# The scan's skip connection on VectorE instead of TensorE in a Mamba-2, attention and mixture-of-experts block

## What is computed

```python
def step(h, inp):                        # per head: 4 heads of 64 channels, 64 states
    x_t, dt_t, B_t, C_t = inp
    dA = jnp.exp(dt_t * A)
    h = h * dA[:, :, None, None] + (dt_t[:, :, None] * x_t)[..., None] * B_t[:, None, None, :]
    y = jnp.einsum('bhpn,bn->bhp', h, C_t)
    return (h, y)
...
y = jnp.moveaxis(ys, 0, 1) + xs * D[None, None, :, None]     # the skip connection
y = y.reshape(Bt, L, D_INNER)
y = y * jax.nn.silu(z)
y = y * jax.lax.rsqrt(jnp.mean(jnp.square(y), axis=-1, keepdims=True) + EPS) * norm_w
return y @ out_proj_w.T
```

## Time and profile before

| | |
|---|---|
| three runs, median (lowest to highest) | 913.11 us (911.67 to 915.75) |
| profiled execution | 912.75 us, of which the span from first to last instruction 911.0 us |
| mean granted PE clock in the span | 0.967 of 2.4 GHz |
| busy: PE, DVE, ACT, POOL | 796.8, 632.1, 502.1, 300.3 us |
| `diag_d` products on PE | 128 records, 22.9 us busy |
| `xdt` products on DVE (L1458) | 32, 13.6 us busy |

### The profile page before, as it was taken

How to read it: one execution, slowest core, us unless ns; L and a number is a source line. 1 busy time by engine, 2 the same in 40 slices (tenths; PEclk the granted TensorE clock), 3 DMA queues, 4 the chain that set the end, 5 groups by cost and what they waited for, 6 DMA issues and landing times.

```text
span 911.0 us, 17953 instructions
## 1 busy us (share of the span) xinstructions
PE 796.8 (87%) x5396; PEld 473.8 (52%) x5396; DVE 632.1 (69%) x1491; ACT 502.1 (55%) x960; POOL 300.3 (33%) x566
## 2 busy tenths in 40 slices
PE   3549999998999889998999899998999989998887
PEld 1324454745547455654546455464556546464545
DVE  1675468784888748885697847886588856977523
ACT  2324675465843675456754667436754567446552
POOL 4322606044231614135150542316151351405300
PEclk9756999999999999999999999999999999999979
DMA  4000000000000000000000000000000000000000
GB/s 157 1 8 12 15 1 1 8 14 24 0 1 6 25 11 0 7 12 24 0 0 7 13 23 0 1 17 24 0 0 7 12 24 0 0 7 13 24 0 12
DMA packets 15144, 11.72 MB, mean 13 GB/s; under 512 B 1040, under 2 KB 13968, under 8 KB 14992
## 3 DMA queue, kind: packets, MB, share of 16 engines
q1 hardware_dynamic: 15120, 11.43, 4.2%
HBM read 7.76 MB, written 2.10 MB: 11 GB/s over the span
## 4 chain that ended last, share of the span: by engine, by line
PE 56%; DVE 17%; issue 12%; ACT 8%; POOL 6%; DVEq 1%; POOLq 0%; ACTq 0%
PE R L443 38%; PE S L443 13%; DVE sb_mx L1176 6%; DVE sb_x L1422 2%; POOL sb_pr L1690 2%; POOL sb_lnv L1595 2%; PE S L448 1%; DVE sb_tokqk L1359 1%; PE R L561 1%; PE R L448 1%; ACT sb_es L1114 1%; ACT L943 1%; ACT sb_junk L989 1%; DVE sb_st L1200 1%; DVE sb_yc L1480 1%
## 5 line engine op out<-in xcount | busy, mean ns | idle before, releaser
L1079 ACT ACTIVATE sb_pr<-S 128x768 f32<-128x768 f32 (+1 forms) x192 | 165.6, 887 | 152.3 <-PE S L443 151.2
L1176 DVE TENSOR_REDUCE sb_mx<-S 128x2 f32<-128x256 f32 (+3 forms) x256 | 198.0, 817 | 37.8 <-PE S L443 35.7
L1690 POOL TENSOR_SCALAR_AFFINE_SELECT sb_pr<-sb_pr 128x256 f32<-128x256 f32 (+1 forms) x192 | 97.0, 507 | 339.6 <-ACT sb_pr L1079 337.6
L443 PE MATMUL R<-sb_pr,sb_va 128*32 128x512 f32 (+3 forms) x1024 | 89.7, 445 | 19.6 <-POOL sb_pr L1690 19.6
L443 PE MATMUL S<-sb_maskb,sb_identb 128*128 128x128 bf16 (+1 forms) x384 | 51.4, 249 | 32.8 <-DVE sb_mx L1176 30.2
L443 PEld LDWEIGHTS S<-sb_maskb,sb_identb 128*128 128x128 bf16 x384 | 27.8, 101 | 100.3 <-DVE sb_mx L1176 83.6
L443 PE MATMUL R<-sb_xfT,sb_W 128*128 128x512 f32 x144 | 75.9, 635 | 3.3 <-ACT sb_pr L943 3.3
L443 PE MATMUL R<-sb_W,sb_pr 128*128 128x96 f32 (+1 forms) x512 | 70.9, 279 | 0.0
L443 PEld LDWEIGHTS R<-sb_W,sb_pr 128*128 128x128 f32 x512 | 62.8, 192 | 4.4 <-issue 3.6
L443 PE MATMUL S<-sb_kT,sb_qT 32*128 32x256 f32 (+3 forms) x512 | 58.9, 403 | 0.0
L443 PE MATMUL S<-sb_qT,sb_kT 32*128 32x256 f32 (+3 forms) x512 | 57.2, 388 | 0.0
(11 more groups left out here) (208 smaller groups left out, 1712.3 us busy)
## 6 DMA issues: line engine op xcount, KB each, us to landing
sb_xin<-x SPq DMA_DIRECT2D x9, 256.0 KB, 2.8
sb_W<-weights SPq DMA_DIRECT2D x1, 2290.0 KB, 10.5
sb_qT<-sb_mT SPq DMA_DIRECT2D x128, 4.0 KB
sb_xres<-x SPq DMA_DIRECT2D x8, 256.0 KB, 2.9
out<-sb_xres SPq DMA_DIRECT2D x7, 256.0 KB, 2.3
sb_cT<-sb_xact SPq DMA_DIRECT2D x8, 128.0 KB, 2.3
sb_W<-weights SPq DMA_DIRECT2D x1, 514.0 KB, 5.1
sb_cst<-consts SPq DMA_DIRECT2D x1, 328.0 KB, 3.2
```

The costliest lines, as they stand in the source:

```text
L443: return pe.matmul(o, lhsT, rhs, start=start, stop=stop, skip_group_check=True)
L1079: act.activation(pr[:, e % 4, :, 0:n], S[pair_of_exp(e)][:, :, 0:n], ACT.Exp).then_inc(p_sb, 1)
L1176: o = dve.tensor_reduce(mx[:, n // P - 1, g, heads[0]:heads[1] + 1], found[:, :, at_col:at_col + n], AX.X, ALU.max, negate=True)
L1690: pool.affine_select(out=keep, in_=keep, compare_op=ALU.is_ge, fill=0.0, base=0, pattern=pattern, channel_multiplier=-1)\
```

## The change

The product `xs * D` moves to DVE. Once at the start PE multiplies a matrix of ones with `diag_d`, which gives a matrix `drow` with D along the free axis, the same in all 128 partitions; DVE copies it from PSUM to SBUF, and PE's transposes wait for that copy. In every chunk, behind `wm`, DVE multiplies the transposed channels in `R[2]` with `drow` into `xd`. In `scan_outputs` the two diagonal products are gone. In `scan_combine` DVE adds `xd`: from chunk 1 on to the decayed state part, in place, ahead of the sum with `R[3]`; in chunk 0 the sum of `R[3]` and `xd` is a new step ahead of `yz`.

```diff
@@ signals
+        drow_ps = signal("drow_ps", 0)
+        drow_set = signal("drow_set", 0)
...
-        yc_sb = signal("yc_sb", 2 * (T - 1))
+        yc_sb = signal("yc_sb", 1 + 3 * (T - 1))
+        xd_sb = signal("xd_sb", T)
@@ PE, scan_outputs
-                for n in range(2):
-                    mm(R[3][:, n * P:(n + 1) * P], xact[:, n, s], diag_d[:, n, :], c == 0 and n == 0, False)
                 for h in range(NH):
                     i = mm(R[3][:, h * HP:(h + 1) * HP], wm[:, c % 2, h, :],
-                           xdt[:, c % 2, h * HP:(h + 1) * HP], False, True)
+                           xdt[:, c % 2, h * HP:(h + 1) * HP], c == 0 and h == 0, True)
@@ PE, start
             pe.wait_ge(dve_set, 7)
+            for n in range(2):
+                i = mm(R[0][:, n * P:(n + 1) * P], ones, diag_d[:, n, :])
+            i.then_inc(drow_ps, 1)
+            pe.wait_ge(drow_set, 1)
             pe.wait_ge(xab_sb, at(xab_sb, -2, 1))
@@ DVE, scan_weights
                    ALU.mult).then_inc(wm_sb, 1)
+                tt(xd[:], R[2][:, 0:DI], drow[:], ALU.mult).then_inc(xd_sb, 1)
@@ DVE, scan_combine
-                if c == 0:
-                    y = R[3][:, 0:DI]
-                else:
+                skip = xd[:]
+                dve.wait_ge(xd_sb, at(xd_sb, r, c + 1))
+                if c > 0:
                     tt(yc[:, 0, :].rearrange("p (h d) -> p h d", h=NH),
...
                         .then_inc(yc_sb, 1)
-                    dve.wait_ge(yc_sb, at(yc_sb, r, 2 * c - 1))
-                    tt(yc[:, 1, :], R[3][:, 0:DI], yc[:, 0, :], ALU.add).then_inc(yc_sb, 1)
-                    dve.wait_ge(yc_sb, at(yc_sb, r, 2 * c))
-                    y = yc[:, 1, :]
+                    dve.wait_ge(yc_sb, at(yc_sb, r, 3 * c - 1))
+                    tt(yc[:, 0, :], yc[:, 0, :], xd[:], ALU.add).then_inc(yc_sb, 1)
+                    dve.wait_ge(yc_sb, at(yc_sb, r, 3 * c))
+                    skip = yc[:, 0, :]
+                tt(yc[:, 1, :], R[3][:, 0:DI], skip, ALU.add).then_inc(yc_sb, 1)
+                dve.wait_ge(yc_sb, at(yc_sb, r, 3 * c + 1))
+                y = yc[:, 1, :]
                 tt(yz[:, c % 2, :], y, zraw[:, c, 0:DI], ALU.mult).then_inc(yz_sb, 1)
@@ DVE, start
             norms(-2)
             dve.wait_ge(dve_set, 7)
+            dve.wait_ge(drow_ps, 1)
+            dve.tensor_copy(drow[:], R[0][:, 0:DI]).then_inc(drow_set, 1)
+            dve.wait_ge(drow_set, 1)
```

More of the change, by code:

```diff
@@ L133, in build @@
         diag_d = sb("diag_d", [P, 2, P])
+        drow = sb("drow", [P, DI])
+        xd = sb("xd", [P, DI])
         def w(name):
```

## The result

The changed kernel takes 934.6 us (932.8 to 937.1, six runs) against 913.35 us (910.8 to 918.3, six runs of the kernel before beside it): a ratio of 1.022, interval 1.018 to 1.027. The forecast was 916.8 us, at most 920.8; the changed kernel takes 18 us more than the forecast. The profiled execution has a span of 932.5 us (before: 911.0).

The account below looks back on a forecast made before the run. The prediction took each chunk to have its own limit among PE, VectorE and GpSimd. Start +1.05, first round +0.4 and seven rounds +2.2 made +3.7 us on the median 913.11: 916.8 us, range 912.0 to 920.8.

Parts of the forecast that it names:

- what bounds the kernel: Opening part: each chunk has its own limit; one full round of about 105.8 us, PE's clock at 1.00, stands for seven.
- Chunk 2: GpSimd's norm chain ends last, so PE's gain only lengthens its 1.06 us wait for the mask: 0 us a round.
- Start and first round: Making `drow` delays PE's transposes once, +1.05 us; the first round, without GpSimd's cover for two normalizations, was given +0.4.
- Chunk 0: VectorE's `xd` (0.34 us) and new addition (0.46) delay the last maximum and PE's next load, partly absorbed: +0.50 us a round.
- Chunk 1: In the path through `scan_outputs` and the combine, PE saves 0.55 us and VectorE's addition costs 0.46: -0.09 us a round.
- the port rival: In chunk 2 VectorE's addition and GpSimd's power step collide on their shared SBUF port: up to 3.4 us, 920.2 us, chance 0.20.
- Chunk 3: PE's `scan_outputs` and VectorE's `yz` follow one another on the path; -0.55 and +0.46 give -0.09 us a round.
- The round's sum: All chunks of a full round together: 0.50 - 0.09 - 0.09 = +0.32 us, over seven rounds +2.2.
- the terms 0.50 + 0.46 + 0.46: VectorE's added work on the path: 0.50 us in the first chunk, 0.46 for the combine's addition in the second and fourth.
- 0.55 + 0.55: PE's saving from the removed diagonal products, 0.55 us in each of the second and fourth chunks of a round.
- PE counts after all: Rival: the combine's addition hidden, the first chunk free, 0.55 us kept twice a round: 905.4 us, chance 0.08.

## Why the prediction was wrong

- **The step that failed** stands in the part on what bounds the kernel and in "Chunk 2. PE's gain lengthens its wait of 1.06 us; the combine ends where it did. 0." The granted clock of 1.00 was taken as a property of the round, and a longer wait of PE as free. In the changed kernel the waits are longer and stretches at 0.50 stand behind them. That term, 17 of the 21 us, was missing, and none of the rivals had it. Shown: useless products in or ahead of the waits take 44 of 54 us of half clock away, at undisturbed rounds of about the same length, and most of it goes at the two masks. Not settled: what decides whether a given round falls. The undisturbed round of the changed kernel has waits of 1.78, 1.24 and 1.32 us and no fall. Their sum does not decide: with chunk 3 filled alone they are 1.78, 1.24 and 0.26 us and six rounds of seven fall, two of them in chunk 0 alone; in the kernel before they are 1.51, 1.06 and 0.66 us and none does. Nor was a wait made longer by itself, with the streams of PE and VectorE as they were; in the runs here the waits grew with one of the two. That the length of the waits brings the falls is therefore argued, not shown.
- **Start and first round**: +1.05 and +0.4 were forecast, +0.95 came in all. PE's first transposes went from 13.10 to 14.37, 0.2 us later than forecast. What the first round itself costs can't be read off: the profiled execution of the changed kernel happened to hold some 44 us of half clock ahead of the first full round, that of the kernel before 48.
- **Chunk 0**: +0.50 forecast, +0.49 measured, by the steps named: the maximum after `xd` at +0.33 (0.34), the next at +0.25 (0.26), PE's load behind the last at +0.49. The last maximum starts 0.62 us later (0.64 forecast), and the load stands 0.06 us behind its end, where it stood 0.18 behind it before. The forecast had these 0.06 without a row for them.
- **Chunk 1**: -0.09 forecast, about -0.02 measured. PE's gain was mis-sized. From the state product's start to the product of L448 behind the weighted ones it is 855.71 - 854.05 = 1.66 us, against 2.10 before (303.46 to 305.56): 0.44, not 0.55, because the eight weighted products now take 1.10 us and not 1.00.
- **Chunk 2**: 0 forecast, -0.10 measured in the undisturbed round; PE's wait there is 1.24 us, not about 1.5. The power step stayed 1.64 us and the addition inside it 0.42, so the port rival did not happen at its place.
- **Chunk 3**: -0.09 forecast, +0.20 measured. The addition took 0.63 us, begun 0.28 us into GpSimd's mask. So the two engines do collide, as the port rival had it, but in another chunk and with another instruction. The Trainium skill, "SBUF — State Buffer", section "SBUF: two separate sides", has whichever engine comes first hold the other off for its whole instruction. The rows of the mask agree in kind (0.63, 0.81 and 0.87 us beside it), but VectorE's operation ends as if it had been held until about 0.5 us into a mask recorded at 0.64; those of the power step (0.42 within it) do not agree.
- **The round's sum**: 0.49 - 0.02 - 0.10 + 0.20 = +0.57, where +0.32 was forecast. With that and a level clock the profiled execution would have stood at 911.0 + 0.95 + 4.0 - 0.6 = 915.4 us of span, near the forecast. That is in part luck: VectorE's side measures 2.02 us a round with PE's whole stream, where the terms 0.50 + 0.46 + 0.46 give 1.42, and PE's side gives 1.45 back, where 0.55 + 0.55 was forecast. Both are too small, and their errors of 0.60 and 0.35 mostly cancel.
- **PE counts after all**: taken alone and with a level clock the products are worth 0.45 us a round, not 1.10, and unfilled nothing at all (ratio 1.003); behind VectorE's added work they are worth 1.45. The Trainium skill, "Perfetto Trace Analysis", section "Identifying the Most-Contended Engine", starts at the engine of highest occupancy, but would not have TensorE judged by the busy share of its products; it names instead the share of the peak rate and the busy share of the weight loads, and the latter is 52%, under VectorE's 69%. So the rule, read whole, does not clearly single out PE, as the prediction has it. In the kernel before, work taken from PE mostly lengthened its waits.

## What to carry over

Where an engine with a gated clock waits at several places of a loop, an edit that lengthens those waits, from either side, can cost more by the clock than by its own duration, as it did in this kernel: look at the granted clock of every round, and ask of each microsecond won or added which wait it goes into. Compare kernels by their undisturbed rounds first and by their stretches of half clock second; here the two had different causes. Useless work put in or ahead of the longest waits, as a test, tells them apart; here it made both kernels faster. Useful work moved there was not tried.

## What was not expected of the hardware

- Six products without use, about 3.2 us of PE's time a round, made a kernel 14.6 us faster (934.6 to 920.0), and four of them the kernel before 3.9 us faster (913.4 to 909.5).
- GpSimd's mask and VectorE's operations on two SBUF inputs slow one another by 0.2 to 0.5 us (the mask 0.88 for 0.40, `yz` 0.87 for 0.43), so that a gain of 0.44 us ahead of such a pair can vanish in it; a power step of 1.64 us slowed no addition inside it.
- The eight weighted products took 1.10 us when the diagonal products no longer preceded them, and 1.00 us behind them.
